# A fused transformer-like stack on one core: the output addition, one wait and the idle products at the start of its wide attention

## The reference, cut to what matters

```python
q = (hidden_states @ wq).reshape(b, s, H, DK).transpose(0, 2, 1, 3)   # H = 16 heads, DK = 64
k = (hidden_states @ wk).reshape(b, s, H, DK).transpose(0, 2, 1, 3)
v = (hidden_states @ wv).reshape(b, s, H, DK).transpose(0, 2, 1, 3)
scores = jnp.einsum('bhqd,bhkd->bhqk', q, k)
bias = rel_emb[buckets].transpose(2, 0, 1)[None]
attn = jax.nn.softmax(scores + bias, axis=-1)
out = jnp.einsum('bhqk,bhkd->bhqd', attn, v)
return out.transpose(0, 2, 1, 3).reshape(b, s, H * DK) @ wo      # and x = x + this
```

## Time and profile before

| | |
|---|---|
| median of 3 runs | 1204.48 us |
| profiled execution, its own time | 1206.97 us |
| its span | 1205.2 us |
| wide attention, from the first projection (50.8) to about 456 | some 405 us |
| TensorE busy in the span | 1145.7 us (95%) |
| VectorE, ScalarE, GpSimd busy | 906.6, 885.3, 609.5 us (75, 73, 51%) |
| mean granted TensorE clock | 0.993 of full speed |

### The profile page before, as it was taken

The page is one execution under the profiler, slowest core; times in us unless marked ns, Lnnn a source line. Parts: engine busy times, 40 slices in busy tenths (PEclk is TensorE's granted clock), DMA queues, the critical chain, the costliest instruction groups (busy, mean ns, idle before and its releaser), DMA issues.

```text
span 1205.2 us, 39867 instructions
## 1 busy us (share of the span) xinstructions
PE 1145.7 (95%) x15770; PEld 697.1 (58%) x15770; DVE 906.6 (75%) x2419; ACT 885.3 (73%) x2390; POOL 609.5 (51%) x402
## 2 busy tenths in 40 slices
PE   7899999999999999799999999988999899999997
PEld 3345555655555554576666666554556566666664
DVE  2498888888889877786777777767677777777773
ACT  5666666666667668787977897777878688877874
POOL 0176665666656553564655564433435355554640
PEclk9999999999999999999999999999999999999999
DMA  5622222222323222310211111110111111110110
GB/s 174 240 61 65 73 65 72 60 78 55 82 56 81 56 56 84 101 42 19 49 41 22 38 43 30 22 29 18 40 27 32 32 28 41 41 41 20 41 41 19
DMA packets 35481, 66.71 MB, mean 55 GB/s; under 512 B 6704, under 2 KB 8176, under 8 KB 35296
## 3 DMA queue, kind: packets, MB, share of 16 engines
q1 hardware_dynamic: 35296, 64.16, 20.2%
HBM read 15.32 MB, written 1.11 MB: 14 GB/s over the span
## 4 chain that ended last, share of the span: by engine, by line
PE 79%; DVE 5%; ACT 5%; issue 4%; DMA 3%; SPq 3%; POOL 1%; DVEq 0%; ACTq 0%; POOLq 0%
PE ps L479 11%; PE ps L458 9%; PE ps L1437 7%; PE ps L1400 5%; PE ps L1367 5%; PE ps L1337 5%; PE ps L1316 5%; PE ps L1306 4%; PE ps L1407 4%; PE ps L1379 4%; PE ps L1307 3%; DMA arena<-arena 2%; PE ps L1443 2%; PE ps L487 2%; PE ps L444 2%
## 5 line engine op out<-in xcount | busy, mean ns | idle before, releaser
L417 POOL TENSOR_TENSOR arena<-arena 128x1024 f32<-128x1024 f32 x128 | 241.4, 1895 | 163.8 <-DVE arena L661 163.8
L568 ACT ACTIVATE arena<-arena 128x512 f32<-128x512 f32 x256 | 182.5, 714 | 118.4 <-DVE arena L647 118.4
L1248 POOL TENSOR_TENSOR arena<-arena 128x1024 f32<-128x1024 f32 x64 | 121.5, 1898 | 230.5 <-DVE arena L1819 230.5
L1641 ACT ACTIVATE arena<-arena 128x128 f32<-128x128 f32 x512 | 198.3, 391 | 30.6 <-DVE arena L1811 30.1
L647 DVE CUSTOM_DVE_ANT_0 arena<-ps,arena 128x512 f32<-128x512 f32 x256 | 164.6, 688 | 30.8 <-PE ps L458 28.0
L1811 DVE CUSTOM_DVE_ANT_0 arena<-ps,near,arena 128x128 f32<-128x128 f32 x512 | 144.4, 346 | 42.2 <-PE ps L1367 42.1
L657 DVE STREAM_TRANSPOSE arena<-arena 128x1024 f32<-128x1024 f32 x128 | 156.6, 1232 | 1.2 <-POOL arena L417 0.9
L479 PEld LDWEIGHTS ps<-arena 32*64 32x64 f32 x8192 | 120.3, 130 | 56.7 <-issue 31.8
L1255 POOL TENSOR_TENSOR arena<-arena 128x1024 f32<-128x1024 f32 x64 | 151.1, 2361 | 0.6 <-PE ps L1337 0.5
L458 PE MATMUL ps<-arena 64*128 64x512 f32 x512 | 142.1, 630 | 5.2 <-issue 3.5
L479 PE MATMUL ps<-arena 32*64 32x128 f32 x8192 | 137.5, 273 | 4.5 <-issue 2.7
(11 more groups left out here) (178 smaller groups left out, 2112.1 us busy)
## 6 DMA issues: line engine op xcount, KB each, us to landing
arena<-arena SPq DMA_DIRECT2D x191, 128.0 KB, 2.4
arena<-arena SPq DMA_DIRECT2D x64, 192.0 KB, 2.6
arena<-rel_rows SPq DMA_DIRECT2D x16, 448.0 KB, 9.0
arena<-arena SPq DMA_DIRECT2D x64, 64.0 KB, 2.1
arena<-y SPq DMA_DIRECT2D x30, 128.0 KB, 2.3
arena<-arena SPq DMA_DIRECT2D x15, 127.8 KB, 2.4
arena<-in_wqkv SPq DMA_DIRECT2D x2, 768.0 KB, 5.2
x<-in_x SPq DMA_DIRECT2D x4, 256.0 KB, 5.6
```

Of the source, the lines that this page charges most:

```text
L417: nc.gpsimd.tensor_tensor(e, e, scale, ALU.mult).then_inc(self.normed, 1)
L568: nc.scalar.activation(self.e[:, r % 3, i, :], self.neg[:, i, :], ACT.Exp, bias=self.nmax[:, i:i + 1], scale=-1.0, accum_out=self.sums[:, ...
L1641: nc.scalar.activation(self.e[:, s, h, :], self.neg[:, h, :], ACT.Exp, bias=self.nmax[:, h:h + 1], scale=-1.0, accum_out=self.sums[:, s, h ...
```

## The change

There are three edits.

```diff
-WARM = 10
+WARM = 4
@@ weigh(u, half), half == 0
                 pe.wait_ge(self.q_read, min(u + 3, self.UNITS))
                 pe.wait_ge(self.k_read, min(u + 3, self.UNITS))
-                pe.wait_ge(self.v_read, min(u + 3, self.UNITS))
+                pe.wait_ge(self.v_read, u + 1)
                 pe.wait_ge(self.v_spread, 96 * (u + 1))
                 pe.wait_ge(self.turned, 4 * (u + 1))
             for c in range(half * blocks // 2, (half + 1) * blocks // 2):
                 for a in range(self.GROUPS):
+                    if c == 0 and a == self.GROUPS - 1:
+                        pe.wait_ge(self.v_read, min(u + 3, self.UNITS))
                     rows = slice(a * self.BLOCK, (a + 1) * self.BLOCK)
@@ dve, the loop over u
             if scores and not closing:
                 turn(r, 0)
                 invert_sums(r + 1, 0)
-                turn(r, 1)
             if u >= 1:
                 add_out(u - 1)
+            if scores and not closing:
+                turn(r, 1)
             if scores:
                 add_bias(r + 1, 2)
```

## The result

| | before | changed |
|---|---|---|
| median on the same chip (7 runs each) | 1205.02 us (1201.17 to 1207.46) | 1197.44 us (1194.3 to 1200.89) |
| ratio | 1 | 0.9943, 95% interval 0.9922 to 0.9964 |
| profiled execution, its own time; its span | 1206.97; 1205.2 us | 1195.92; 1194.1 us |

A forecast was written before the change was run, and what follows sets the result against it. TensorE was taken to bound the kernel. Breaks -12.7, tail -1.0, addition -1.8 and start +1.0 gave -14.5 us: profiled 1206.97 to 1192.5, median 1190.0 us predicted, range 1186.5 to 1197.

The forecast's parts named there:

- The bound and the blocks: Wide attention: TensorE sets the pace, and its breaks come from its program arriving in blocks of 256 instructions.
- So the seven turns lose their breaks: Wide attention: with 24 fewer instructions at the start, block ends move to places without breaks, gaining 12.7 us.
- The later wait for the values' copy: First weigh half: moving this wait to the product needing it was worth nothing by itself.
- up to +1.8: Weigh products: a wait carried inside them could cost up to 0.06 us each, +1.8 us in all.
- The addition, -1.8: Attention turns: the addition ahead of the transposition removes TensorE's wait of 0.06 to 0.07 us, 29 times: 1.8 us less.
- The tail, -1.0: Last weigh half of the attention: the block's end there moves later and its 1.03 us idle goes, 1.0 us less.
- The start, +1.0: First normalisation: with fewer early products TensorE is still at 1.2 GHz, costing 1.0 us; bounds -0.7 to +3.4.
- The rivals: Three: breaks stay (8%), 3.8 us pairs too short (13%), cold start costs more than everything gains (1211 us, 5%).
- The first (breaks stay): Attention: breaks repeat for some reason other than blocks and remain; only -0.8 us, 1203.7 us; chance 8%.
- the second: Attention: block-end pairs 3.8 us apart are too short and lose up to 0.2 us each; 1195.6 us; chance 13%.

The follow-up runs named there:

- e8: Kernel before with 4 products on zeroed memory, not 10, and the values' projection's second product waiting for this turn's L487 product: 1192.78 us against 1205.40.
- e1: Kernel before with only the six products on zeroed memory taken away (4 left of 10): 1212.03 us against 1203.88.
- e7: Kernel before with only the later wait for the values' copy, 10 products, addition still behind the transposition: 1199.09 us against 1205.40.
- e6: Kernel before with only the addition moved ahead of the transposition, 10 products: 1203.82 us against 1205.40, ratio 0.9994.
- e5: Kernel before, 10 products kept, with 40 instructions that only wait added ahead of the attention: 1214.02 us against 1205.40.
- e9: Changed kernel with a wait on the values' projection's second product, as in e4, but on a semaphore long reached: 1194.57 us.
- e4: Changed kernel in which the second product of the values' projection also waits for this turn's L487 product: 1188.81 us against the kernel before's 1203.88.
- e11: Changed kernel with queries' and keys' copy waits also moved from the weigh step's head to the first product needing each: 1191.23 us against the kernel before's 1203.71.
- e12: As e11, but with 10 products on zeroed memory: 1190.04 us against the kernel before's 1203.71, ratio 0.9878.
- e10: As e4, but with 10 products on zeroed memory and 40 waiting instructions ahead of the attention: 1192.84 us against the kernel before's 1206.08.

## Why the prediction was wrong

- *The bound and the blocks.* Right. TensorE sets the pace, its program comes in blocks of 256 instructions, and in every trace but e8's breaks stand at such ends. The Trainium skill, "Runtime: NRT & Kernel Launch", section "Instruction fetch mechanics", has the blocks of 256 too, which agrees; that crossing into the next is mostly hidden does not, since up to 13.9 us of breaks stand in these traces.
- *"From 15, the eighth weigh MATMUL, to 143 ... no break. ... All other pairs cover the projections and take far longer. So the seven turns lose their breaks."* This is the step that failed. The pair from 143 (in L431) to 271 (the 112th MATMUL of the weigh half) does take longer, 5.2 us, and breaks all the same. The step rests on "the next block is ready some 3.6 to 3.8 us after the last end". It is ready 2.2 to 3.0 us after its transfer begins, and when that is depends on whether the stream is held. The prediction counted TensorE's arrays, and the stream runs ahead of them. Gained were 9.4 us in the profile, not 12.7, and not by the move of the ends: e1, which has that alone, loses 8 us in the median, and its breaks are 13.9 us.
- *The later wait for the values' copy: "I take nothing for it by itself."* Wrong, and it is the edit that pays: by its ratio -5.9 us in e7 alone, of which 4.6 are shorter breaks in the profile. The prediction looked at who is last for the arrays, although the order of instructions had shown that three of them only wait there. The price inside the fast products, up to +1.8, isn't there: plain turns are at 11.75.
- *The addition, -1.8.* The size was right in the profile: 11.81 to 11.75 in each turn, and e6's attention is 2.2 us shorter. In the median of e6 it doesn't show (ratio 0.9994, 0.9982 to 1.0007), so as time of the kernel it isn't shown.
- *The tail, -1.0.* Right in size: L753 follows at 439.70 without a gap, and the last turn is 0.7 us shorter.
- *The start, +1.0.* The first products ran at half speed as forecast (3.78 us for four MATMULs). From them to the next MATMULs of L128 it was 4.42 us before (11.41 to 15.83) and 4.52 now (10.57 to 15.09); in the seven kernels with 4 products it is 4.42 to 5.33, but it is 5.33 in e5 and e7 with 10 products too. So up to 0.9 us are lost there, and 0.1 in this profile. Further on no cost shows: with 4 products the first weigh half begins at 71.6 to 74.0 us, with 10 between 70.5 and 75.0 (e5 and its 40 waits at 76.8).
- *Profile against median.* The forecast with the breaks that were left would be -14.5 + 3.3 = -11.2 us, and the profiled executions differ by 11.1. That they agree so closely is partly luck, since -2.7 us ahead of the attention and +3.1 behind it happen to cancel. The medians differ by 7.6. Part of this is the clock: the profiled execution was at a mean of 0.992, and of the seven the three at 0.992 to 0.994 took 1194.3 to 1197.0 us, the four at 0.989 to 0.991 took 1197.4 to 1200.9. How many of the seven ends are late wasn't seen but in the one profile, and e9's shows one; what stands in the other executions, and why the stretches at 0.50 change, is open.
- *The sum itself.* With all breaks gone e4 gains 0.0119 of 1205, 14.3 us. The terms of the forecast were those of a kernel whose blocks are asked for in time, which the changed kernel was at four of these seven ends.

The rivals: none came true. The first (breaks stay) had the right effect for the wrong reason, the second had the size (1195.6 us) by another mechanism, pairs of 3.8 us, of which none broke in the changed kernel. The rival that was missing is "the breaks move with the ends", and e1 and e5 are its price.

## What to carry to other kernels

Where an engine gets through 256 instructions in 2.5 to 3 us, ask not only what its arrays wait for but what its instruction stream waits for: an instruction that only waits, placed ahead of work that is already covered, can cost nothing in the row of waits and still delay the next block. Let each wait be carried by the first instruction that needs it. Before moving block ends by adding or removing instructions elsewhere, take the hold away: with it gone (e11, e12) the places no longer mattered in the 29 full turns, though up to 0.6 us stayed in the closing ones.

## What was not expected of the hardware

- A block's transfer begins 1.8 to 3.2 us before TensorE's arrays reach the end of the last block if the stream is free (e12), 0.9 to 1.6 us after it if three waiting instructions stood just before it (before), and 3.5 to 4.9 us after it if the stream ran past the end into such a hold (the late ends of changed and e1). The block is usable 2.2 to 3.0 us after its transfer begins.
- A waiting instruction of its own stands in the trace with the time that it holds the stream: 3.6 us in each turn of the changed kernel, while TensorE's arrays have no idle time at all in a clean one.
- Of e1's seven ends at this place all were late, of the changed kernel's three, of e9's one, of e4's, e8's, e10's and e11's none. That the same program is late at some ends and not at others is shown; what decides it isn't, though the time of the transfer before sorts 20 of 21 ends.
- TensorE at half speed in the first normalisation cost 0.1 us at the next step in the changed kernel's profile, and nothing that can be seen in the time of the whole. The column of the granted clock has 1.00 there (10.80 to 13.80, where four MATMULs fill 3.00 us) because the trace has no clock record ahead of 14.3 us.
